# Graph attention layers of a GNN + FFN kernel on Trainium2: scores, softmax and edge sums joined into one stage of four chunks

## Chip, cores and metric

The kernel runs on one core of one Trainium2 chip. The metric is device time in microseconds (us) of one execution, the median of several.

## What is computed

A graph of 3125 nodes and 53,125 directed edges (sorted by destination) with 256 features per node passes through one attention layer, a routed FFN, three graph attention (GAT) layers with a small MLP behind them, and a second routed FFN. The change touches the three GAT layers. Their reference, cut to what matters:

```python
def _gat(x, src, dst, W, a_src, a_dst, b, heads, out_ch, concat):
    h = (x @ W).reshape(n, heads, out_ch)
    al_s = jnp.einsum('nhc,hc->nh', h, a_src)
    al_d = jnp.einsum('nhc,hc->nh', h, a_dst)
    e = jax.nn.leaky_relu(al_s[src] + al_d[dst], 0.2)
    emax = jax.ops.segment_max(e, dst, num_segments=n)
    ee = jnp.exp(e - emax[dst])
    denom = jax.ops.segment_sum(ee, dst, num_segments=n)
    alpha = ee / (denom[dst] + 1e-16)
    out = jax.ops.segment_sum(h[src] * alpha[:, :, None], dst, num_segments=n)
    ...
h = elu(_gat(x, ..., 4 heads of 128, concatenated))   # layer 1
h = elu(_gat(h, ..., 4 heads of 128, concatenated))   # layer 2
h = _gat(h, ..., 1 head of 256)                       # layer 3
```

## The kernel before

Nodes lie in 25 tiles of 128. Edges are cut into 232 items (ITEMS): an item is two sub-blocks of 128 edges whose destinations fall in one node tile, whose number stands in the table `item_tile`. Two consecutive items are called a pair here (116 pairs; `groups` in the code). Every GAT layer runs five phases, each with a barrier of all engines behind it: dense (node rows h and the scores of the nodes), scores, edges (which begins with the softmax), nodes, and then the next layer's dense phase.

**Scores** (`phase_gat_scores`, L1616), a rolled loop over the 116 pairs. Each engine works in its own order and they meet at semaphores. SP loads the low parts of the source and destination numbers, repeated on 128 partitions, four items at a time and four such buffers ahead (L1647). DVE compares them with the partition number to get one-hot matrices (L1739) and every second pair builds one-hots of the source tile (L1736). PE multiplies one-hots with the node scores, which are cut into three bf16 parts: 12 matmuls of 100 columns (25 tiles x 4 heads) for the sources (L1689) and 12 of 8 columns for the destination (L1693), on four PSUM banks and four further ones. The table of the destination tile is copied by POOL for one item (L1672) and by ACT for the other (L1708). DVE masks the 400 results (L1747) and reduces them (L1753); ACT copies the destination's scores (L1712).

**Softmax**, the head of `phase_gat_edges` (L1759): PE transposes all scores, DVE runs a segmented maximum forwards and backwards over 512 columns per head (L1863 to L1893), with PE transposes between for the carry over partitions, then DVE forms the shifted exponents (L1901 to L1910) and ACT takes exp (L1837). Meanwhile ACT clears `acc` (L1834), the 25 x 522 sums, and POOL starts the gathers.

**Edges**, an unrolled loop over the 232 items. POOL gathers 2 x 128 rows of the table in DRAM with two indirect DMAs an item (L1827) into a ring of 12 items (layer 3: 24), and waits for the sum of the item that had the slot. ACT writes the weights behind the rows (L1844) and weighs two of four heads (L1850); DVE weighs the other two (L1928) and builds the one-hots of the destinations every four items (L1922). PE sums the item with the one-hots (L1816): 2 pieces of 261 columns x 2 sub-blocks, fp32, for the 521 columns of layers 1 and 2 (512 features, 4 weights, 4 maxima, 1 flag); 1 piece of 259 in layer 3. DVE adds the sum to the item's node tile (L1937), three items behind, for which it first loads the tile's number into a register (L1932). Four sums may be open:

```python
            for t in range(ITEMS + LAG):        # DVE, LAG = 3
                if t < ITEMS:
                    weigh(t)
                if t >= LAG:
                    add(t - LAG)
```

No planner sets the order; on each engine it is that of the code.

## Time and profile before

| | us |
|---|---|
| median of 3 runs | 5496.4 |
| lowest, highest | 5494.01, 5509.8 |
| profiled execution: its own time | 5452.6 |
| profiled execution: span from first to last instruction | 5450.9 |

The page of the profile counts PE busy for 71% of the span, DVE for 53%, POOL for 41% and ACT for 33%. The three GAT layers lie between about 1800 and 4740 us of the span. Views used below: the windows view (busy time of each engine in a stretch), groups of instructions by line, timelines of one engine, waits, and one line's instructions. "DVEq" stands for instructions that DVE's sequencer carries out by itself, which don't count as busy. A number in parentheses after an x is a count.

### The profile page before, as it was taken

The numbers are of one execution on the slowest core, as the hardware profiler recorded it, in microseconds if no ns is written. First come the engines' busy times: TensorE is split into PE (matmuls) and PEld (weight loads), VectorE is DVE, ScalarE is ACT, GpSimd is POOL, SyncE is SP. The second block draws the span as 40 slices with busy tenths as digits, with TensorE's granted clock in tenths as the row PEclk, the third lists the DMA queues.
The fourth block names the chain that finished last, engine by engine and source line by source line (L and its number), as shares of the span: only waits on it lengthen the run. The fifth ranks groups of instructions, "written<-read, shape, count | busy, mean of one in ns | idle before, by whom it ended". The sixth has DMA issues, their size and how long they took to land. (4 is left out here: it accounts for less than half of the span.)

```text
span 5450.9 us, 85101 instructions
## 1 busy us (share of the span) xinstructions
PE 3889.5 (71%) x22668; PEld 3121.2 (57%) x22669; DVE 2871.4 (53%) x6524; ACT 1797.9 (33%) x5670; POOL 2234.9 (41%) x2473
## 2 busy tenths in 40 slices
PE   5577776887997684777778667777664443667996
PEld 3455555686886474656546656556563322456885
DVE  4577777432002696555567955555784443662112
ACT  0566675221221224444422254444230000021221
POOL 0656663002221025666611356666037777502221
PEclk9788888988998767888888678888856665778998
DMA  2666663004556464666634556665373333304555
GB/s 80 180 180 180 187 186 106 17 25 153 181 185 156 129 172 130 182 183 182 183 114 133 155 149 184 181 181 166 109 215 91 91 91 94 89 29 160 185 182 168
DMA packets 348485, 782.46 MB, mean 144 GB/s; under 512 B 52869, under 2 KB 156908, under 8 KB 339692
## 3 DMA queue, kind: packets, MB, share of 16 engines
q0 software_dynamic: 145920, 459.41, 29.5%
q1 hardware_dynamic: 202348, 320.55, 18.8%
q8 instruction: 88, 1.44, 0.1%
q14 instruction: 129, 1.06, 0.1%
HBM read 729.52 MB, written 50.26 MB: 143 GB/s over the span
## 5 line engine op out<-in xcount | busy, mean ns | idle before, releaser
L1827 POOL DMA_INDIRECT h<-h_table,src_of x1392 | 1420.3, 1020 | 665.8 <-issue 387.6
L1816 PE MATMUL ps<-h,gat_edges_work 128*128 128x261 f32 x3712 | 978.9, 428 | 381.8 <-DVE h L1928 259.4
L1816 PEld LDWEIGHTS ps<-h,gat_edges_work 128*128 128x128 f32 x3712 | 782.1, 214 | 578.4 <-DVE h L1928 205.9
L1937 DVE TENSOR_TENSOR acc<-acc,ps 128x522 f32 (+1 forms) x696 | 418.4, 601 | 919.0 <-remote 596.7
L1850 ACT ACTIVATE h<-h,gat_shared 128x128 f32<-128x128 f32 x1856 | 592.7, 390 | 655.5 <-DMA h<-h_table,src_of 637.2
L724 POOL DMA_INDIRECT edges_rows<-kv_table,src_of x464 | 456.3, 983 | 415.5 <-DVE edges_out_rows L823 160.6
L1816 PE MATMUL ps<-h,gat_edges_hot 128*128 128x259 f32 x928 | 314.9, 495 | 344.1 <-DVE h L1928 179.3
L1928 DVE TENSOR_TENSOR h<-h,gat_shared 128x512 f32<-128x512 f32 x696 | 481.3, 693 | 38.3 <-DMA h<-h_table,src_of 37.2
L1816 PEld LDWEIGHTS ps<-h,gat_edges_hot 128*128 128x128 f32 x928 | 204.7, 240 | 453.9 <-DVE h L1928 168.8
L1325 DVE TENSOR_TENSOR moe_experts_result<-ps,moe_experts_b 128x512 f32<-128x512 f32 x64 | 44.3, 692 | 788.9 <-PE ps L929 788.9
L918 PE MATMUL ps<-moe_experts_turned,moe_experts_w 128*128 128x256 f32 x2048 | 455.9, 381 | 0.0
L929 PE MATMUL ps<-moe_experts_w,acc 128*128 128x256 f32 x2048 | 452.2, 379 | 0.0
L968 ACT ACTIVATE acc<-ps,moe_experts_b 128x256 f32<-128x256 f32 x512 | 214.5, 470 | 691.5 <-PE ps L918 662.1
L1672 POOL COPY gat_scores_of_item<-gat_scores_parts 128x24 bf16 (+1 forms) x348 | 101.0, 290 | 801.5 <-issue 486.9
L929 PEld LDWEIGHTS ps<-moe_experts_w,acc 128*128 128x128 f32 x2048 | 389.1, 190 | 52.9
L918 PEld LDWEIGHTS ps<-moe_experts_turned,moe_experts_w 128*128 128x128 f32 x2048 | 387.5, 192 | 50.7
L788 PE MATMUL ps<-edges_out_rows,h 128*128 128x264 f32 x928 | 308.5, 464 | 126.3 <-DVE edges_out_rows L823 107.4
L1342 POOL DMA_INDIRECT picked_out<-moe_experts_result,moe_slot_out x128 | 125.1, 978 | 635.7 <-DVE moe_experts_result L1325 616.2
L1335 POOL DMA_INDIRECT moe_experts_rows<-normed,moe_slot_in x128 | 124.2, 970 | 636.6 <-POOLq L206 576.0
L778 PE MATMUL ps<-h 128*128 x928 | 294.2, 448 | 103.0 <-issue 70.3
L1689 PE MATMUL ps<-gat_scores_parts,gat_scores_hot 128*128 128x100 bf16 (+1 forms) x4176 | 280.6, 228 | 116.6 <-DVE gat_scores_hot L1739 79.1
L1844 ACT COPY h<-gat_shared 128x18 f32<-128x18 f32 (+1 forms) x696 | 131.2, 193 | 565.9 <-remote 315.7
(349 smaller groups left out, 5709.8 us busy)
## 6 DMA issues: line engine op xcount, KB each, us to landing
moe_experts_w<-in_L_ffn_W SPq DMA_DIRECT2D x128, 1024.0 KB
gat_scores_rows<-src_rows SPq DMA_DIRECT2D x174, 256.0 KB, 3.8
gat_scores_rows<-dst_rows SPq DMA_DIRECT2D x174, 256.0 KB, 4.4
h<-h_table,src_of POOLq DMA_INDIRECT x1392
edges_dst_row<-dst_rows SPq DMA_DIRECT2D x58, 256.0 KB
h_table<-h SPq DMA_DIRECT2D x10, 1280.0 KB
h<-h_table SPq DMA_DIRECT2D x10, 1280.0 KB
h<-picked_out SPq DMA_DIRECT2D x48, 256.0 KB, 3.7
```

The lines of the kernel that those rows point to most:

```text
L724: nc.gpsimd.indirect_dma_start(rows[:, r, s, :], None, k.kv_table, bass.IndirectOffsetOnAxis(ap=k.src_of[:, 2 * t + s:2 * t + s + 1], axis ...
L778: mm = nc.tensor.matmul(psq[r % S][:, s * C:(s + 1) * C], hot_t[:, r % SH, s * P:(s + 1) * P], row(k.h, n, 0, C), start=True, stop=True)
L788: mm = nc.tensor.matmul(pso[r % S][:, 0:W], hot[:, r % S, s * P:(s + 1) * P], out_rows[:, r % S, s, :], start=(s == 0), stop=(s == 1))
L918: mm = nc.tensor.matmul(psh[q][:, j % 2 * GROUP:j % 2 * GROUP + m], f.w1[:, w, b, j * P:(j + 1) * P], f.turned[:, slot, b, 0:m], start=(b ...
L929: mm = nc.tensor.matmul(pso[slot][:, s * C:(s + 1) * C], f.hidden[:, slot, j, s * P:(s + 1) * P], f.w2[:, w, j, :], start=(j == 0), stop=( ...
L968: last = act.activation(f.hidden[:, slot, j, 0:m], k.ps[2 + q][:, j % 2 * GROUP:j % 2 * GROUP + m], ACT.Gelu, bias=e(j))
L1689: nc.tensor.matmul(bank[slot][:, s * HT:(s + 1) * HT], hot[:, slot, 0, s * P:(s + 1) * P], parts[:, p, 0:HT], start=(p == 0), stop=(p == 2))
L1816: mm = nc.tensor.matmul(k.ps[t % S * 2 + q][:, 0:PIECE], hot[:, t // BATCH % 3, t % BATCH * 2 + e, :], g.rows[:, t % RING, e, q * PIECE:(q ...
L1827: nc.gpsimd.indirect_dma_start(g.rows[:, r, e, 0:W], None, g.table, bass.IndirectOffsetOnAxis(ap=k.src_of[:, 2 * t + e:2 * t + e + 1], axis=0)
L1850: last = act.mul(cols, cols, g.sums[:, 2 * t + e, h:h + 1])
L1928: v.tensor_tensor(heads(t, 0, by_dve), heads(t, 0, by_dve), alpha.to_broadcast([P, 2, by_dve, D]), ALU.mult).then_inc(weighed, 1)
L1937: v.tensor_tensor(acc, acc, k.psum[:, t % S * 2:t % S * 2 + PIECES, 0:PIECE], ALU.add).then_inc(added, 1)
```

## The change

The phases scores and edges of a layer become one phase, `phase_gat_layer`, with the same sums in another order. Its 232 items are cut into chunks of 64 (64, 64, 64, 40).

- **Front.** Before the first item, the 32 pairs of chunk 0 are scored and its softmax is run in 20 small steps, of which PE, ACT and DVE do parts in turn. ACT now clears `acc` before it copies the first table of a pair (L1828, L1797). It copies both tables of a pair; POOL copies none.
- **Loop.** While the items of a chunk are summed, the next chunk is scored: one pair in three of four iterations, so that 32 pairs take 43 items. One-hots are built two iterations ahead, PE multiplies in the iteration, and DVE takes the results two behind. The softmax of that chunk takes its 20 steps in the last 20 items. The weights stand in two halves that alternate by chunk.
- **Scores.** Two PSUM banks instead of eight, two row buffers instead of four, three one-hot buffers instead of four. DVE, not ACT, copies the destination's scores (L1872).
- **Sums.** Layers 1 and 2: PE sums 512 columns and then the 9 last ones apart, four items side by side in a bank of their own. DVE adds the 512 columns per item (L1989), and every four items the four tails of 9 columns, each behind its own register load (L1993, L1996). Layer 3 has no tail, six open sums instead of four, and LAG 5.
- **Between chunks.** A node whose edges lie in two chunks needs a maximum over both: the maximum so far is carried on, and at each of three boundaries DVE rescales one node tile of `acc` by a factor (about ten small operations, one exp on ACT and one matmul).
- All loops of the phase are unrolled.

The diff, cut to its core:

```diff
+    BATCH, HOTS, HS, NB = 4, 3, 3, 2
+    S = 4 if TAIL else 6
+    LAG = S - 1
+    CH, E = 64, P
+    CHUNKS, PAIRED = -(-ITEMS // CH), ITEMS // 2
...
+    def scored(t):
+        if t < 0:
+            c, j = 0, t + CH
+        else:
+            c, j = t // CH + 1, (3 * (t % CH) + 2) // 4 if t % 4 < 3 else CH
+        q = c * CH // 2 + j
+        return q if 0 <= j < CH // 2 and q < PAIRED else None
+    def softmax_step(t):
+        c, n = (0, t + CH // 2 - 1) if t < 0 else (t // CH + 1, t % CH - CH + 20)
+        return (c, n) if c < CHUNKS and 0 <= n < 20 else (c, None)
...
+            def sum_item(t):
+                if t % BATCH == 0:
+                    pe.wait_ge(marked, t // BATCH + 1)
+                pe.wait_ge(weighed, t + 1)
+                pe.wait_ge(scaled, t + 1)
+                if t >= S:
+                    pe.wait_ge(added, t - S + 1)
+                if TAIL and t % BATCH == 0 and t >= 2 * BATCH:
+                    pe.wait_ge(tails_added, t // BATCH - 1)
+                for e in range(2):
+                    mm = nc.tensor.matmul(k.ps[t % S][:, 0:MAIN], hot[:, t // BATCH % HOTS, t % BATCH * 2 + e, :],
+                                          g.rows[:, t % RING, e, 0:MAIN], start=(e == 0), stop=(e == 1))
+                if TAIL:
+                    for e in range(2):
+                        mm = nc.tensor.matmul(k.ps[S + t // BATCH % 2][:, t % BATCH * TAIL:(t % BATCH + 1) * TAIL],
+                                              hot[:, t // BATCH % HOTS, t % BATCH * 2 + e, :],
+                                              g.rows[:, t % RING, e, MAIN:FULL], start=(e == 0), stop=(e == 1))
+                mm.then_inc(summed, 1)
...
+            def products(q):
+                c = q // (CH // 2)
+                pe.wait_ge(lo_hots, q + 1)
+                pe.wait_ge(chosen, q + 1)
+                if q >= 2:
+                    pe.wait_ge(masked, q - 1)
+                    pe.wait_ge(dst_taken, q - 1)
+                if c >= 1:
+                    pe.wait_ge(maxed, c)
+                if c >= 2:
+                    pe.wait_ge(factored, c - 1)
...
+            pe.wait_ge(cut, 1)
+            for t in range(-CH, ITEMS):
+                if t >= 0:
+                    sum_item(t)
+                q = scored(t)
+                if q is not None:
+                    products(q)
+                c, n = softmax_step(t)
+                if n is not None:
+                    softmax(c, n)
...
+            def choose(q):
+                if q >= 4:
+                    act.wait_ge(made, q - 3)
+                for j in range(2):
+                    n = act.value_load(k.item_tile[0:1, 2 * q + j:2 * q + j + 1], min_val=0, max_val=TILES - 1)
+                    last = act.copy(of_item[:, q % 4, j, :, :], tables(n))
+                last.then_inc(chosen, 1)
...
+            act.wait_ge(cut, 1)
+            act.wait_ge(noughts, 1)
+            act.copy(k.acc[:, :, 0:FULL], nought[:].rearrange("p (t a) -> p t a", t=1).to_broadcast([P, TILES, FULL])).then_inc(cleared, 1)
+            for t in range(-CH - 2, ITEMS):
+                q = scored(t + 2)
+                if q is not None:
+                    choose(q)
...
+            def one_hots(q):
+                b, at = q // 2, q % 2
+                dve.wait_ge(row_in[b % NB], (b // NB + 1) * 32)
+                if q >= HS:
+                    dve.wait_ge(made, q - HS + 1)
+                if at == 0:
+                    v.tensor_tensor(tile_hot[:, b % 4], k.iota_row[:, 0:TILES].rearrange("p (a n) -> p a n", a=1).to_broadcast([P, 8, TILES]),
+                                    k.src_hi[:, 8 * b:8 * b + 8].rearrange("p (s a) -> p s a", a=1).to_broadcast([P, 8, TILES]),
+                                    ALU.is_equal)
+                v.tensor_scalar(lo_hot[:, q % HS, :, :], rows_lo[:, :, b % NB, at * 512:(at + 1) * 512], k.iota_p[:, 0:1], None,
+                                ALU.is_equal).then_inc(lo_hots, 1)
...
+            def take_scores(q):
+                b, at, j = q // 2, q % 2, 4 * (q % (CH // 2))
+                dve.wait_ge(lo_hots, q + 1)
+                dve.wait_ge(made, q + 1)
+                if q >= 2:
+                    dve.wait_ge(picks, q - 1)
+                v.tensor_tensor(picked[:, q % 2], bank[q % 2][:, 0:4 * HT].rearrange("p (s h n) -> p s h n", s=4, h=H),
+                                tile_hot[:, b % 4, at * 4:at * 4 + 4].rearrange("p s (a n) -> p s a n", a=1).to_broadcast([P, 4, H, TILES]),
+                                ALU.mult).then_inc(masked, 1)
+                v.tensor_copy(g.of_dst[:, :, j:j + 4], bank[q % 2][:, 4 * HT:4 * HT + 8 * H].rearrange("p (s h) -> p h s", s=4)
+                              ).then_inc(dst_taken, 1)
+                dve.wait_ge(masked, q + 1)
+                v.tensor_reduce(g.of_src[:, :, j:j + 4].rearrange("p h s -> p s h"), picked[:, q % 2], AX.X, ALU.add).then_inc(picks, 1)
...
+            def rescale(c):
+                n = dve.value_load(k.item_tile[0:1, c * CH:c * CH + 1], min_val=0, max_val=TILES - 1)
+                dve.wait_ge(factored, c)
+                dve.wait_ge(added, c * CH)
+                if TAIL:
+                    dve.wait_ge(tail_link, c * CH)
+                for h in range(H):
+                    v.tensor_scalar(row(k.acc, n, h * D, (h + 1) * D), row(k.acc, n, h * D, (h + 1) * D), factor[:, h:h + 1], None, ALU.mult
+                                    ).then_inc(rescaled, 1)
+                v.tensor_tensor(row(k.acc, n, W, W + H), row(k.acc, n, W, W + H), factor[:], ALU.mult).then_inc(rescaled, 1)
+                dve.wait_ge(rescaled, (H + 1) * c)
...
             def add(t):
+                if t == 0:
+                    dve.wait_ge(cleared, 1)
+                elif t % CH == 0:
+                    rescale(t // CH)
                 n = dve.value_load(k.item_tile[0:1, t:t + 1], min_val=0, max_val=TILES - 1)
                 dve.wait_ge(summed, t + 1)
                 if t:
                     dve.wait_ge(added, t)
-                acc = k.acc[:, bass.ds(n, 1), 0:PIECES * PIECE].rearrange("p a (q c) -> p (a q) c", q=PIECES)
-                v.tensor_tensor(acc, acc, k.psum[:, t % S * 2:t % S * 2 + PIECES, 0:PIECE], ALU.add).then_inc(added, 1)
-
-            for t in range(ITEMS + LAG):
-                if t < ITEMS:
+                v.tensor_tensor(row(k.acc, n, 0, MAIN), row(k.acc, n, 0, MAIN), k.ps[t % S][:, 0:MAIN], ALU.add).then_inc(added, 1)
+            def add_tails(b):
+                for i in range(BATCH):
+                    n = dve.value_load(k.item_tile[0:1, b * BATCH + i:b * BATCH + i + 1], min_val=0, max_val=TILES - 1)
+                    if b * BATCH + i:
+                        dve.wait_ge(tail_link, b * BATCH + i)
+                    v.tensor_tensor(row(k.acc, n, MAIN, FULL), row(k.acc, n, MAIN, FULL),
+                                    k.ps[S + b % 2][:, i * TAIL:(i + 1) * TAIL], ALU.add).then_inc(tail_link, 1)
+                dve.wait_ge(tail_link, BATCH * (b + 1))
+                dve.sem_inc(tails_added, 1)
+            for t in range(-CH - 2, ITEMS + LAG):
+                if 0 <= t < ITEMS:
                     weigh(t)
+                q = scored(t + 2)
+                if q is not None:
+                    one_hots(q)
+                q = scored(t - 2)
+                if q is not None:
+                    take_scores(q)
+                c, n = softmax_step(t)
+                if n is not None:
+                    softmax(c, n)
                 if t >= LAG:
                     add(t - LAG)
+                    if TAIL and (t - LAG) % BATCH == BATCH - 1:
+                        add_tails((t - LAG) // BATCH)
```

What stands in a row on DVE, in the loop of layers 1 and 2. `h` is the ring of gathered rows, `acc` the sums, `ps` PSUM, ISA a sequencer's instruction. Before, one item, weighed and (another, three behind) added:

```order
L1928 TENSOR_TENSOR h<-h,gat_shared 128x2x256
L1932 TENSOR_LOAD item_tile
L1932 ISA x2
L1937 ISA
L1937 TENSOR_TENSOR acc<-acc,ps 128x522
```

The same engine now, behind the weighing (L1965), in an iteration in which a pair is scored and four tails are due:

```order
L1860 TENSOR_SCALAR gat_layer_lo_hot<-gat_layer_rows_lo,iota_p 128x1024
L1869 TENSOR_TENSOR keys<-ps,gat_layer_tile_hot 128x400
L1872 COPY gat_shared<-ps 128x8x4
L1875 TENSOR_REDUCE keys<-keys 128x4x4
L1985 TENSOR_LOAD item_tile
L1985 ISA x2
L1989 ISA
L1989 TENSOR_TENSOR acc<-acc,ps 128x512
L1993 TENSOR_LOAD item_tile
L1993 ISA x2
L1996 ISA
L1996 TENSOR_TENSOR acc<-acc,ps 128x9
```

Between the weighing and the add stand the three steps of the pair (four with L1857 in every second pair); the last four rows stand there four times before the next weighing.

ACT at the start of the layer. Before, the clearing of `acc` stands behind the scores of the whole layer:

```order
L1708 COPY gat_scores_of_item<-gat_scores_parts 128x24
L1712 COPY gat_shared<-ps 128x8x4 x3
L203 UNCONDITIONAL_BRANCH
L1831 UNCONDITIONAL_BRANCH
L1834 COPY acc<-gat_edges_nought 128x25x522
```

Now:

```order
L1788 UNCONDITIONAL_BRANCH
L1828 COPY acc<-gat_layer_nought 128x25x521
L1797 TENSOR_LOAD item_tile
L1797 ISA x2
L1798 ISA
L1798 COPY gat_layer_of_item<-gat_layer_parts 128x24
```

The clearing has moved ahead of the first table, which PE needs for the first pair.

## Rows read from the trace of the kernel before

**Rows 1.** Windows view: window, its length, busy us (count) of each engine, PE clock, DMA.

```profile
core 0: us, PE busy (x) PEld busy (x) DVE busy (x) ACT busy (x) POOL busy (x), PEclk, DMA share, GB/s
1878.00:2053.00 175.00, 143.74 (x2784) 137.75 (x2784) 173.20 (x405) 47.52 (x229) 37.33 (x115) 0.69 0.64 169
2053.00:2112.00 59.00, 10.15 (x48) 8.03 (x48) 48.22 (x74) 19.17 (x9) 31.25 (x24) 0.53 0.38 107
2112.00:2766.00 654.00, 489.13 (x1848) 391.52 (x1849) 354.18 (x516) 316.50 (x1156) 434.85 (x440) 0.86 0.63 177
...
3942.00:4055.00 113.00, 89.28 (x2781) 83.38 (x2778) 104.46 (x404) 39.20 (x230) 28.57 (x112) 0.50 0.85 259
4055.00:4080.00 25.00, 5.05 (x24) 2.73 (x22) 17.42 (x31) 8.25 (x14) 19.52 (x18) 0.50 0.31 89
4080.00:4731.00 651.00, 314.94 (x928) 204.75 (x928) 294.95 (x521) 41.06 (x223) 465.75 (x447) 0.67 0.32 90
```

**Rows 2.** Windows view, two stretches of layer 3's edges: DVE nearly idle, DVE full.

```profile
4120.00:4170.00 50.00, 8.39 (x17) 4.74 (x17) 6.32 (x11) 0.98 (x5) 38.12 (x40) 0.50 0.36 104
4195.00:4219.00 24.00, 19.11 (x80) 13.19 (x78) 24.00 (x45) 3.77 (x20) 19.55 (x15) 1.00 0.29 83
```

**Rows 3.** Timeline, layer 3: start, us, engine, line, what [idle before <-releaser].

```profile
4158.71 2.10 PE L1816 MATMUL ps<-h,gat_edges_hot 128*128 128x259 f32 x4 [9.11 <-ACT h L1844]
4168.82 0.42 DVE L1937 TENSOR_TENSOR acc<-acc,ps 128x259 f32 x1 [10.17 <-remote]
```

**Rows 4.** Timeline of DVE in layer 1's edges, items at hand.

```profile
2500.47 0.69 DVE L1937 TENSOR_TENSOR acc<-acc,ps 128x522 f32 x1
2501.07 0.71 DVE L1928 TENSOR_TENSOR h<-h,gat_shared 128x512 f32<-128x512 f32 x1
2501.71 0.69 DVE L1937 TENSOR_TENSOR acc<-acc,ps 128x522 f32 x1
```

**Rows 5.** Line L1932, 2498 to 2500 us: durations min/median/max ns, first and last start.

```profile
L1932 DVEq TENSOR_LOAD <-item_tile x2: 300/301/302, 2498.2 to 2499.1; - x2
L1932 DVEq FUSED_REGOPS  x2: 190/190/190, 2498.5 to 2499.4; - x2
L1932 DVEq SEQ_ASSERT  x2: 23/23/23, 2498.8 to 2499.6; - x2
```

**Rows 6.** Groups by line, layer 1's scores: count, busy us, mean ns, idle before.

```profile
L1747 DVE TENSOR_TENSOR acc<-ps,acc 128x400 f32<-128x400 f32 x116 | 65.6, 566 | 0.7 <-PE ps L1693 0.5
L1753 DVE TENSOR_REDUCE keys<-acc 128x400 f32 (+1 forms) x116 | 64.7, 559 | 0.0
L1739 DVE TENSOR_SCALAR gat_scores_hot<-gat_scores_rows,iota_p 128x1024 bf16<-128x1024 bf16 x116 | 55.3, 477 | 0.0
L1736 DVE TENSOR_TENSOR acc<-iota_row,src_hi 128x200 f32<-128x200 f32 x57 | 20.2, 354 | 0.6 <-DMA gat_scores_rows<-dst_rows 0.6
```

**Rows 7.** Groups by line and form, whole span.

```profile
L1834 ACT COPY acc<-gat_edges_nought 128x13050 f32<-128x13050 f32 x2 | 22.1, 11070 | 6.0 <-DVE gat_edges_nought L1856 6.0
...
L1873 DVE COPY gat_edges_cin<-ps 128x16 f32<-128x16 f32 x1 | 0.2, 175 | 0.7 <-PE ps L1800 0.7
```

**Rows 8.** Timeline of PE: a pair's 24 matmuls at half clock and at full clock.

```profile
1904.44 1.08 PE L1689 MATMUL ps<-gat_scores_parts,gat_scores_hot 128*128 128x100 bf16 x12 [0.17 <-DVE gat_scores_hot L1739]
1905.36 0.44 PE L1693 MATMUL ps<-gat_scores_of_item,gat_scores_hot 128*128 128x8 bf16 x12
...
1907.24 0.70 PE L1689 MATMUL ps<-gat_scores_parts,gat_scores_hot 128*128 128x100 bf16 x12 [0.47 <-DVE gat_scores_hot L1739]
1907.78 0.45 PE L1693 MATMUL ps<-gat_scores_of_item,gat_scores_hot 128*128 128x8 bf16 x12
```

**Rows 9.** Timeline of PE in a dense phase at full clock: fp32, 8 and 512 columns.

```profile
2858.22 0.95 PE L606 MATMUL ps<-gat_wa,gat_shared 128*128 128x8 f32 x8
2859.50 3.60 PE L606 MATMUL ps<-gat_w,gat_shared 128*128 128x512 f32 x8
```

**Rows 10.** Groups by line, DVE, layer 1's edges.

```profile
L1922 DVE TENSOR_TENSOR gat_edges_work<-iota_row,dst_in 128x1024 f32<-128x1024 f32 x57 | 69.7, 1223 | 0.0
```

457 lines of the change are left out of this document (201 added, 256 removed).

## The prediction, made before the changed kernel ran

> **What bounds the kernel now.** I read the windows view first. A GAT layer of four heads spends 175 us on scores, 59 us on the softmax and 654 us on the edges; layer 3 spends 113, 25 and 651 us [rows 1]. Layer 2 I take as layer 1. The reader should see three different limits. In the scores DVE is busy for 173.2 of 175 us. In the softmax DVE is busy for 48.2 of 59, and the other 11 are hand-overs between PE and DVE. In the edges no engine is full: PE 489, DVE 354, POOL 435 of 654 us. POOL is still the nearest: at its full pace it issues 40 gathers in 50 us [rows 2], 1.25 us each, so 464 of them need 580 us. When DVE is busy without a break, 15 gathers take 24 us [rows 2], 1.6 us each. The rest of the 2.82 us per item is a delay between PE and its readers: PE's four matmuls of an item start at 4158.71 and last 2.10 us, yet DVE's next add, which waits for a sum of PE, starts at 4168.82 after 10.17 us of idleness [rows 3]. So DVE has 300 of 654 us to spare in the edges, and the change wants to put the 234 us ahead of them there.
>
> **The front, layers 1 and 2.** It holds 32 pairs and one softmax.
> - ACT's clearing of acc (11.07 us [rows 7]) stood under the softmax. It now stands ahead of the first table, and PE cannot begin without one: +13 us with the table's load and copy.
> - A pair cost 175/116 = 1.5 us, DVE's own work. Now two PSUM banks close a loop. DVE masks pair q (0.57 us [rows 6]) and copies the destination's scores (PSUM to SBUF, 0.175 [rows 7]), which frees the bank, 0.66 with overlap; PE starts 0.2 later and needs 1.0 us at full or 1.4 at half clock for 24 matmuls [rows 8]; only then may DVE build the next one-hots (0.48, and half of 0.35 [rows 6]), 0.55, and with 0.1 for the signal the next mask follows. That is 2.5 to 2.9 us a pair; I take 2.75, nearer the half clock, since PE waits half the time: 32 x 2.75 = 88 us. Bounds: 48 us at the old pace, 96 at 3.0.
> - Softmax of 128 columns: a quarter of 48 us, 2 us of fixed cost for forty small operations, the same 11 us of hand-overs, 1 for exp: 26 us.
> Together 127 us against 234: **-107 us** a layer.
>
> **The loop, layers 1 and 2.** DVE's work for four items:
> - Weighing and adding: two steps of 0.6 us (the adds start at 2500.47 and 2501.71 [rows 4]), 4 x 1.24 = 5.0 us.
> - The destination's one-hots, 1.22 [rows 10] less overlap: 1.15.
> - Four tails. The add of 9 columns itself is some 0.15 us. But each stands behind a load of the tile's number, of which the sequencer's parts take 0.30, 0.19 and 0.02 us, and two loads in a row start 0.9 us apart with nothing in their way (2498.2 and 2499.1 [rows 5]). Today this lies under the 0.7 us weighing. With four loads behind one another nothing is left for DVE to do: 4 x 0.88, less what the add of 512 columns covers, 3.1 us. Bounds: 0.7 if all is hidden, 3.7 if nothing.
> - Three pairs: 0.57 + 0.56 + 0.48 + 0.18 (half of L1736) + 0.17 (the copy that ACT made) [rows 6, 7] less overlap of 0.3 is 1.65 each, 5.0. The reduce waits for the mask, and the add's register load comes after it, 0.9 us against 0.6 of reduce: 0.3 each, 0.9.
> Sum 15.1 us, 3.75 an item while a pair is scored, and 9.2/4 = 2.3 while none is. PE needs 4 x (4 x 0.45 + 4 x 0.12) [rows 9] + 3 x 1.0 = 12.1 us at full clock, 14 at the 0.86 of these edges [rows 1], so it stays just behind DVE. ACT and SP gain work too, with room left: ACT had 316 of 654 us, and a pair adds two loads and two copies, about 2 us.
>
> The layer then: chunks 0 and 1, each 43 items x 3.75 = 161 us, and 21 x 2.3 = 48 with 25 for the softmax (14 of work, 8 of waits for PE, which answers only behind its item, 3 for the rescaling factor), 234 each, 468. Chunk 2: 27 x 3.75 = 101; 17 items at 2.9, POOL's pace beside a busy DVE, 49; 20 x 2.3 + 25 = 71; 221. Chunk 3: 40 x 2.95 = 118. Three rescalings of a tile, each with a stop until all adds are in, 9. Sum 816 us against 654: **+162 us**. With the front +55 a layer, **+110** for two.
>
> **Layer 3.** There is no tail. Front: clearing half as large, 7 us; a pair 1.9 us by the same loop with quarter-sized masks, 61; softmax 22; 90 against 138, -48. Loop: DVE needs under 2.4 us an item even with pairs, below POOL's 2.5, so POOL bounds. The moved work is 84 pairs of 104.5/116 = 0.9 us [rows 1] and 24 us of softmax, some 100 us of DVE; each busy us of DVE slows POOL by 1 - 1.25/1.6 = 0.22: +24, and +7 for rescaling. **-17 us.** Three barriers fall away, 2 us each: **-6 us.**
>
> Sum: 110 - 17 - 6 = **+87 us**. The profiled execution took 5452.6 us (span 5450.9) and the median is 5496.4; I add the change to both: 5540 profiled, 5583 as a median. I say **5580 us**.
>
> **The shared port.** In the rows POOL's gather goes from 1.25 to 1.6 us beside a full DVE [rows 2]; that is the price used above. The Trainium skill, SBUF — State Buffer, section "A bandwidth-pool intuition that's wrong", has a harder rule: a DVE operation that takes both ports locks POOL out of writing descriptors until it ends. By that rule it is the new one-hots in the loop (one source, bf16) that count, not DVE's total. The rows agree with a slowdown and don't show its form for this operation. As a mechanism here, each of 84 one-hots of 0.48 us [rows 6] that stops POOL adds 40 us a layer where POOL bounds, layer 3: rival E.
>
> **Rivals.**
> - **A (forecast, 0.52).** DVE bounds the loops of layers 1 and 2: 5580, own range 5500 to 5690.
> - **B (0.22), faster: the register loads are hidden.** If DVE has a backlog when the tails come, since PE or a gather was late, they cost 0.7 and not 3.1 us. Scoring items then take 3.2, the others POOL's 2.8 to 2.9: 199 + 199 + 192 + 112 + 9 = 711 us, 838 with the front, -50 a layer: 5496 - 100 - 23 = 5373. Against it: the tails stand behind the iteration in which DVE has most to do, and the loads 0.9 us apart are in the trace.
> - **C (0.07).** The front's pairs keep 1.5 us and the loops are as forecast: 2 x 40 and 30 in layer 3 less: 5470.
> - **D (0.13), slower still: the late signal of PE.** The 8 us in [rows 3] fell on an idle DVE. DVE now also waits in the same order for PE's products and transposes. If a delay of 8 us falls on one in five groups of four items, 1.5 us each, 58 groups in each of two layers give +175, and the front some 20: 5780. For it: every second wait of the softmax is of this kind. Against it: in stretches where DVE is busy and POOL slower the delay is not seen, and that is what the loop will be.
> - **E (0.06).** Descriptors starve in layer 3: 5620.
>
> **How the numbers follow.** The range leaves out at most the faster half of B and the slower half of D: 5385 to 5790. It takes in both bounds of the tail (0.7 to 3.7 us per four) together with those of the front. A change of 0.3%, 16 us, is about what a measurement can tell. Faster: B, most of C and a little of A, 0.26. Within: 0.10. Slower: 0.64. More of it is on the slow side because DVE alone, with no other wait, needs about 880 of today's 888 us of a layer: the former busy time of 173 + 48 + 354 = 575, 33 for copies and tails, 160 for the register loads, and the stops in front and softmax.
>
> **What the profile will show.** Right: the layers of four heads some 940 us from first pair to last add; DVE idle before the adds of 9 columns (L1996) for about 0.7 us each, put down to nothing that waits; pairs 2.5 to 2.9 us apart in the front; DVE idle before L1860 there, released by PE; 11 us without PE at the start. Wrong: adds of 9 columns back to back (then B), ring waits of POOL gone in layers 1 and 2, PE fuller than DVE in the loops, or idle DVE before L1869 and L1989 for 8 us at a time (then D). The forecast falls if the loop of layers 1 and 2 takes under 720 us.

## The result, and the profile of the changed kernel

The changed kernel takes 5674.2 us (median of 4 runs, 5652.27 to 5681.25), the kernel before 5503.1 (4 runs): a ratio of 1.030, 95% interval 1.0265 to 1.034. It is slower by 171 us where the prediction said 87: the direction was right, the size was half. The profiled execution took 5675.8 us. That of the kernel before had been 50 us below its median, so the two traces differ by 223 us; I read places from them, and the size from the medians.

Windows view of the changed kernel, one row each for the front (to the first weighing) and the loop of layers 1, 2 and 3. The answer to [rows 1].

```profile
core 0: us, PE busy (x) PEld busy (x) DVE busy (x) ACT busy (x) POOL busy (x), PEclk, DMA share, GB/s
1888.00:2028.00 140.00, 50.72 (x780) 46.95 (x780) 70.57 (x182) 28.00 (x70) 22.06 (x24) 0.50 0.41 112
2028.00:2886.00 858.00, 681.46 (x3914) 403.47 (x3914) 582.12 (x1266) 340.43 (x1331) 453.93 (x440) 0.88 0.56 160
3045.00:3185.00 140.00, 50.56 (x780) 46.96 (x780) 70.85 (x184) 26.82 (x69) 21.86 (x23) 0.50 0.37 113
3185.00:4053.00 868.00, 686.83 (x3914) 404.00 (x3914) 583.03 (x1265) 339.99 (x1331) 451.33 (x440) 0.88 0.55 158
4176.00:4312.00 136.00, 27.55 (x774) 24.40 (x774) 43.64 (x171) 18.55 (x70) 45.09 (x48) 0.50 0.44 117
4312.00:4954.00 642.00, 431.92 (x2968) 303.34 (x2968) 408.06 (x992) 60.37 (x403) 451.58 (x416) 0.67 0.42 119
```

Fronts: 140, 140, 136 (forecast 127, 127, 90). Loops: 858, 868, 642 (forecast 816, 816, 682). In no stage is an engine full: in the loop of layer 1 DVE works 582 of 858 us and PE 681. Two kinds of idleness fill the rest.

**The first is the one forecast.** DVE in layer 1's loop: the end of an iteration in which a pair is scored and four tails are due.

```profile
2115.22 0.69 DVE L1989 TENSOR_TENSOR acc<-acc,ps 128x512 f32 x1 [0.25 <-issue]
2116.02 0.17 DVE L1996 TENSOR_TENSOR acc<-acc,ps 128x9 f32 x1
2116.80 0.17 DVE L1996 TENSOR_TENSOR acc<-acc,ps 128x9 f32 x1 [0.61 <-DVE acc L1996]
2117.57 0.17 DVE L1996 TENSOR_TENSOR acc<-acc,ps 128x9 f32 x1 [0.61 <-DVE acc L1996]
2118.35 0.17 DVE L1996 TENSOR_TENSOR acc<-acc,ps 128x9 f32 x1 [0.61 <-issue]
2118.66 0.69 DVE L1965 TENSOR_TENSOR h<-h,gat_shared 128x512 f32<-128x512 f32 x1
```

Four additions of 0.17 us stand 0.78 us apart, behind their register loads.

**The second stands where no term of the forecast was.** Layer 3's front, timelines of PE, DVE and ACT, and the windows view of 47 us of it:

```profile
4182.80 0.27 PE L1748 MATMUL ps<-gat_layer_of_item,gat_layer_lo_hot 128*128 128x2 bf16 x5
4183.72 0.16 PE L1748 MATMUL ps<-gat_layer_of_item,gat_layer_lo_hot 128*128 128x2 bf16 x1 [0.64 <-issue]
4185.15 0.20 PE L1748 MATMUL ps<-gat_layer_of_item,gat_layer_lo_hot 128*128 128x2 bf16 x2 [1.28 <-issue]
4186.61 0.20 PE L1748 MATMUL ps<-gat_layer_of_item,gat_layer_lo_hot 128*128 128x2 bf16 x2 [1.26 <-issue]
4188.05 0.16 PE L1748 MATMUL ps<-gat_layer_of_item,gat_layer_lo_hot 128*128 128x2 bf16 x1 [1.23 <-issue]
4188.74 0.19 PE L1748 MATMUL ps<-gat_layer_of_item,gat_layer_lo_hot 128*128 128x2 bf16 x1 [0.53 <-issue]
4244.17 0.48 PE L1744 MATMUL ps<-gat_layer_parts,gat_layer_lo_hot 128*128 128x25 bf16 x12 [55.23 <-DVE gat_shared L1872]
```

```profile
4195.28 0.48 DVE L1860 TENSOR_SCALAR gat_layer_lo_hot<-gat_layer_rows_lo,iota_p 128x1024 bf16<-128x1024 bf16 x1 [12.77 <-remote]
4242.97 0.37 DVE L1857 TENSOR_TENSOR gat_layer_tile_hot<-iota_row,src_hi 128x200 f32<-128x200 f32 x1 [47.21 <-remote]
```

```profile
4195.82 0.20 ACT L1798 COPY gat_layer_of_item<-gat_layer_parts 128x6 bf16 x1 [13.51 <-remote]
...
4243.51 0.20 ACT L1798 COPY gat_layer_of_item<-gat_layer_parts 128x6 bf16 x1 [46.87 <-remote]
```

```profile
4188.00:4235.00 47.00, 0.35 (x2) 0.10 (x1) 0.48 (x1) 0.40 (x2) 35.72 (x38) 0.50 0.40 116
```

In the second pair PE's matmuls begin to come in ones and twos, every 1.4 us, with nothing named that they wait for, and DVE and ACT stand still for 47 us, until 4243. POOL meanwhile issues its 48 first gathers, one each 1.25 us; its last starts at 4234.46. The trace also has the time of every semaphore update. The first pair's last matmul is recorded at 4182.5 and its signal at 4195.2; the second pair's at 4188.7 and its signal at 4242.9, 54 us later and 7.5 us after the last gather has ended. Where between these two times PE really works the trace doesn't tell. I call this "PE held": the records of matmuls far apart, or their signal late. In layers 1 and 2, where the ring is 24 gathers long, the first masking comes 36 us after the phase's start.

### The profile page after: what moved, and what is told of

It is laid out like the page before. It is cut to its first block and busy times, and to the rows that moved or that the text cites. A ratio compares the mean times of both kernels' runs of the same rounds, so it can differ in the third digit from the quotient of the medians.

```text
span 5674.0 us, 83659 instructions
## 1 busy us (share of the span) xinstructions
PE 4132.1 (73%) x22686; PEld 2996.0 (53%) x22687; DVE 3057.7 (54%) x7636; ACT 1756.6 (31%) x5685; POOL 2162.9 (38%) x2124
## 5 line engine op out<-in xcount | busy, mean ns | idle before, releaser
L1706 POOL DMA_INDIRECT h<-h_table,src_of x1392 | 1448.6, 1041 | 1748.3 <-PE ps L1726 811.4
L1722 PE MATMUL ps<-h,gat_layer_hot 128*128 128x512 f32 (+1 forms) x2784 | 1445.3, 655 | 563.8 <-DVE h L1965 344.6
L1722 PEld LDWEIGHTS ps<-h,gat_layer_hot 128*128 128x128 f32 x2784 | 581.1, 231 | 938.9 <-issue 464.4
L1989 DVE TENSOR_TENSOR acc<-acc,ps 128x512 f32 (+1 forms) x696 | 414.9, 596 | 254.6 <-issue 126.7
L1965 DVE TENSOR_TENSOR h<-h,gat_shared 128x512 f32<-128x512 f32 x696 | 478.3, 688 | 30.2 <-DMA h<-h_table,src_of 11.8
L1798 ACT COPY gat_layer_of_item<-gat_layer_parts 128x24 bf16 (+1 forms) x696 | 145.9, 219 | 1104.5 <-PE ps L1748 465.0
L1726 PEld LDWEIGHTS ps<-h,gat_layer_hot 128*128 128x128 f32 x1856 | 321.6, 216 | 278.8 <-issue 278.8
L1744 PE MATMUL ps<-gat_layer_parts,gat_layer_lo_hot 128*128 128x100 bf16 (+1 forms) x4176 | 255.0, 215 | 252.3 <-DVE gat_shared L1872 147.8
L1744 PEld LDWEIGHTS ps<-gat_layer_parts,gat_layer_lo_hot 128*128 128x128 bf16 x4176 | 235.0, 113 | 288.2 <-DVE gat_layer_lo_hot L1860 195.5
L778 PEld LDWEIGHTS ps<-h 128*128 128x128 f32 x928 | 207.9, 232 | 188.8 <-issue 150.9
```

Of the source, the lines that this page charges most:

```text
L778: mm = nc.tensor.matmul(psq[r % S][:, s * C:(s + 1) * C], hot_t[:, r % SH, s * P:(s + 1) * P], row(k.h, n, 0, C), start=True, stop=True)
L1706: nc.gpsimd.indirect_dma_start(g.rows[:, r, e, 0:W], None, g.table, bass.IndirectOffsetOnAxis(ap=k.src_of[:, 2 * t + e:2 * t + e + 1], axis=0)
L1722: mm = nc.tensor.matmul(k.ps[t % S][:, 0:MAIN], hot[:, t // BATCH % HOTS, t % BATCH * 2 + e, :], g.rows[:, t % RING, e, 0:MAIN], start=(e ...
L1726: mm = nc.tensor.matmul(k.ps[S + t // BATCH % 2][:, t % BATCH * TAIL:(t % BATCH + 1) * TAIL], hot[:, t // BATCH % HOTS, t % BATCH * 2 + e, :],
L1744: nc.tensor.matmul(bank[q % 2][:, i * HT:(i + 1) * HT], lo_hot[:, q % HS, 0, i * P:(i + 1) * P], parts[:, p, 0:HT], start=(p == 0), stop=( ...
L1965: v.tensor_tensor(heads(t, 0, by_dve), heads(t, 0, by_dve), alpha.to_broadcast([P, 2, by_dve, D]), ALU.mult).then_inc(weighed, 1)
```

## Two kinds of batches

The experiments ran in six batches (the expectations say "call"), each with the kernel before in it and each on one chip. In four batches the kernel before took 5466 to 5510 us; I call them A, and the runs of the result (5503) are like them. In two it took 5176 and 5177: B. What differs isn't shown. It isn't simply which chip it is: e1, e2, e3 and e6 ran on the chip that the record numbers 4, in B, and 27 minutes later c2 and e1_again on number 4, in A. Groups by line, DVE, whole span: the same addition, in a phase ahead of the GAT layers that the change doesn't touch, in the changed kernel (A) and in e3 below (B).

```profile
L833 DVE TENSOR_TENSOR acc<-acc,ps 128x264 f32 x232 | 97.5, 420 | 157.3 <-issue 130.1 <-remote 20.8 <-DVE edges_out_rows L823 2.8
```

```profile
L833 DVE TENSOR_TENSOR acc<-acc,ps 128x264 f32 x232 | 97.3, 419 | 1.3 <-DVE acc L833 0.8 <-PE ps L788 0.5
```

157 us of waiting in A, 1.3 in B, at equal busy time: in B PE isn't held. The kinds give the experiments a second axis. No trace of the kernel before was taken in B. Front and loop of each layer in us, from DVE's first instruction of the phase to the first L1965 and from there to the last L1989 (the lines' own timelines):

| kernel | kind | ratio to before | layer 1 | layer 2 | layer 3 |
|---|---|---|---|---|---|
| changed | A | 1.030 | 142, 857 | 142, 868 | 137, 642 |
| e1_again: gathers behind front | A | 1.031 | 128, 880 | 128, 880 | 84, 703 |
| e2_again: tails without loads | A | 1.003 | 142, 787 | 141, 775 | 135, 635 |
| e6_again: four edits | A | 0.975 | 93, 775 | 93, 775 | 73, 648 |
| e1 | B | 1.017 | 128, 793 | 128, 788 | 86, 614 |
| e2 | B | 0.981 | 123, 720 | 124, 726 | 87, 576 |
| e3: six front banks | B | 0.997 | 98, 789 | 97, 789 | 77, 577 |
| e4: e1 and e2 | B | 0.991 | 128, 724 | 128, 723 | 84, 620 |
| e5: four edits, late gathers | B | 0.972 | 93, 723 | 92, 723 | 74, 616 |
| e6 | B | 0.968 | 93, 720 | 93, 727 | 72, 583 |

The changed kernel itself never ran in a batch of kind B. It can be estimated: e3's 5156 us plus the fronts of e2 in place of its own (25 + 28 + 10) is 5219; e1 and e2 corrected in the same way give 5213 and 5210. That is an estimate of some +40 us, 1.007 to 1.008, where A has +171.

## Experiments

**The kernels unchanged (c0, c1, c2, c3, c4).**

c0, the kernel before: 

> The kernel before, unchanged, for its trace beside the experiments, which ran at 5176 us for it where 5496 was measured first. Theory (in the first traces PE's signals came late whenever POOL issued gathers unbroken, and here they don't): the edges of layer 3 take 580 to 600 us instead of 651, bounded by POOL's 1.25 us a gather (464 x 1.25 = 580), and DVE has no idleness of 10 us before L1937. Rival (the difference is PE's granted clock alone, 0.86 against 0.82): edges of layer 3 at 640 or more with the same 10 us stops.

Measured: a batch of kind A, 5519.2 us; layer 3's edges 675 us and 39 stops of DVE of over 4 us before its adds, together 319 us. The delay of [rows 3] came in every trace of A. A third trace of the kernel before, c3 (5472 us, also A), has 32 such stops, 270 us.

c1, the changed kernel: 

> The changed kernel, unchanged, to stand beside the experiments on the same chip. If the ratio of 1.030 holds: 5330 us. If the late signals of PE made part of both kernels' times and hit the kernel before more, the ratio grows: fronts of 122 us, loops of 790 us in layers 1 and 2 and 580 in layer 3 give 5260 us, 1.016.

c2: 

> The changed kernel once more, in the same call as the next run. Where the kernel before takes 5499 us: 5664, the fronts' first masking 36, 36 and 69 us after their start. Where the kernel before takes 5176: first maskings 17, 17 and 13 us after the start, loops of 790, 790 and 577 us (as in the single edits), 5245 us, a ratio of 1.013; if the ratio is 1.029 there too, 5327, the late signals are no part of the loss.

c4: 

> The changed kernel in the same call. Where the kernel before takes about 5500 us: 5665. Where it takes 5176: from the stages of the single edits (fronts of 123, 124 and 87 us in e2, loops of 789, 789 and 577 us in e3) e3's time of 5156 plus 25, 28 and 10 us for the fronts, 5219, a ratio of 1.008.

Measured, all three in A: 5664, 5662 and 5673 us, ratios 1.029 (1.0265 to 1.0312), 1.030 (1.0281 to 1.0321) and 1.0315 (1.0279 to 1.0352). The result repeats to 0.3%. What was expected of c1 (5330 or 5260) was worked out for a batch like that of the first experiments, B, and it ran in A.

**e1: does POOL's burst hold PE?** One edit:

```diff
         def _(pool):
+            pool.wait_ge(exped, 1)
             for t in range(ITEMS):
```

In B: 

> The changed kernel with one edit: POOL waits for the exponentials of chunk 0 before its first gather, in each of the three layers. Theory (PE is held while POOL issues gathers one behind another and DVE stands still): the first masking (L1869) comes 14 us after the first one-hots of the front instead of 35 in layers 1 and 2 and instead of 60 in layer 3, so the fronts shrink from 140, 140 and 136 us to about 120, 120 and 80; some 5 us a layer come back at the first item, whose rows now arrive late. Sum about -80 us. Rival (the stop comes from something else at the start of the phase, such as the clearing or code that isn't there yet): the fronts stay and the kernel gets 15 us slower.

Measured: 5260.8 us, ratio 1.017 (1.015 to 1.0184). The first masking comes 17, 17 and 11 us after the start. But in e2 and e3 of the same batch, whose gathers start at once, it comes at 17, 17 and 13 us too: in B there was nothing to win, and layer 3's loop loses 37 us for its late rows (614 against 577).

In A, beside the unchanged kernel: 

> The changed kernel with POOL's first gather behind the exponentials of chunk 0, beside the unchanged one. Where the kernel before takes 5499 us, theory (unbroken gathers hold PE): first maskings 17, 17 and 11 us after the start, fronts 19 + 19 + 50 us shorter, 5664 - 85 = 5580. Rival (what delays PE there isn't POOL): 5680, fronts unchanged. Where the kernel before takes 5176: 15 us slower than the changed kernel, since the first rows only come later.

Measured: 5672.6 us, ratio 1.031, the changed kernel beside it 1.030. The time is the rival's, the fronts are the theory's: the first masking comes at 17, 17 and 11 us, and the fronts are shorter by 14, 14 and 53 us. What neither foresaw is that the loops grew by 26, 15 and 62 (c2's are 854, 864, 641). Windows view of e1_again, layer 3's front and the 72 us behind it, and DVE in these:

```profile
4177.00:4261.00 84.00, 26.88 (x774) 23.91 (x774) 44.50 (x178) 19.86 (x77) 5.18 (x4) 0.50 0.46 125
4261.00:4333.00 72.00, 16.68 (x116) 10.29 (x116) 7.96 (x21) 1.29 (x8) 49.64 (x51) 0.52 0.35 101
```

```profile
4283.10 0.41 DVE L1858 TENSOR_TENSOR gat_layer_tile_hot<-iota_row,src_hi 128x200 f32<-128x200 f32 x1 [14.04 <-remote]
...
4332.21 0.49 DVE L1861 TENSOR_SCALAR gat_layer_lo_hot<-gat_layer_rows_lo,iota_p 128x1024 bf16<-128x1024 bf16 x1 [46.09 <-remote]
```

The stops of 13 and 47 us went with the burst: 14 and 46 us, now at the first items. So in A the burst makes them, and moving it moves them. In B the same burst of 48 gathers, 1.25 us apart and beside an idle DVE (layer 3's front in e3), makes none.

**e9, e10: does DVE's idleness belong to it?** 40 needless compares on DVE, first behind DVE's first wait for PE (e9, at `q == 0` ahead of the first masking), then ahead of it (e10, shown):

```diff
+                if q == 3:
+                    for i in range(40):
+                        if i >= 3:
+                            dve.wait_ge(busy, i - 2)
+                        v.tensor_tensor(hot[:, i % 3], ..., ALU.is_equal).then_inc(busy, 1)
                 if q is not None:
                     one_hots(q)
```

e9: 

> The changed kernel with 40 needless compares of 1024 columns (1.2 us each, 47 us) on DVE ahead of the first masking of every layer, while POOL issues its first gathers. Where the kernel before takes 5499 us: ACT's fifth table (it waits for PE's first pair) comes 22, 22 and 14 us after the fourth now, the seventh (it waits for the second pair) 1.2, 1.2 and 48 us after the fifth. Theory (PE is held only while DVE is idle): both come within 3 us, since DVE is busy. Rival (POOL's burst holds PE whatever DVE does): they come as late as now, or later still, since POOL is slower beside a busy DVE: its 48 gathers last 77 instead of 60 us. Time: 3 x 47 less what the stops took (19 + 19 + 56), 5710, or 5790 to 5820 by the rival. Where the kernel before takes 5176 the tables come within 3 us anyway.

Measured: 5778.5 us, both stops as before (12.9 and 46.2 us in layer 3). It tells nothing: the fourth pair's one-hots (L1861 there) wait for PE and stand ahead of the compares, so these ran when the burst was over.

e10: 

> The changed kernel with 40 needless compares of 1024 columns on DVE, 47 us, now right behind the third one-hots of every front and so ahead of DVE's first wait for PE, while POOL issues its first gathers. What is read: when ACT copies the tables of the fifth pair (they wait for PE's first pair) and of the sixth (PE's second pair). In the changed kernel, where the kernel before takes 5499 us, they come 22 and 23 us after those of the fourth pair in layers 1 and 2, 14 and 61 us after in layer 3. Theory (PE is held while DVE is idle): both within 3 us of the fourth pair's. Rival (POOL's burst holds PE whatever DVE does): both at 15 us or later, in layer 3 the sixth at 50 us or later. Where the kernel before takes 5176 they come within 3 us in any case.

Measured, in A beside c4, one run: 5701.2 us. After the fourth pair's last table those of the fifth and sixth pairs come at 1.7 and 3.2 us (layer 1), 1.7 and 3.0 (layer 2), 4.5 and 5.8 (layer 3); in c4 at 21.5 and 22.7, 21.6 and 22.8, 17.1 and 61.3. Three of the six are past the 3 us that the theory asked for, but all are far from the rival's 15. Layer 3 of e10, DVE and ACT, and a window in which the compares run:

```profile
4198.21 45.49 DVE L2010 TENSOR_TENSOR gat_layer_hot<-iota_row,dst_in 128x1024 f32<-128x1024 f32 x40
```

```profile
4202.16 0.20 ACT L1799 COPY gat_layer_of_item<-gat_layer_parts 128x6 bf16 x1 [4.30 <-PE ps L1749]
4202.78 0.20 ACT L1799 COPY gat_layer_of_item<-gat_layer_parts 128x6 bf16 x1 [0.42 <-issue]
4203.42 0.20 ACT L1799 COPY gat_layer_of_item<-gat_layer_parts 128x6 bf16 x1 [0.43 <-issue]
```

```profile
4199.00:4247.00 48.00, 1.41 (x31) 1.11 (x30) 46.32 (x46) 0.80 (x4) 41.30 (x23) 0.50 0.25 71
```

While DVE computes no signal of PE comes late; ACT no longer waits 47 us. Three times 45.5 us of needless work, 136, cost 28. In layer 3 the same front shows the other half as well. The compares end at 4243.7 with 22 gathers still to come, POOL goes on at 1.25 us each until 4270, and DVE, idle again, stands for 22 us until PE's next signal:

```profile
4271.52 0.37 DVE L1858 TENSOR_TENSOR gat_layer_tile_hot<-iota_row,src_hi 128x200 f32<-128x200 f32 x1 [22.43 <-remote]
```

So the theory holds for the fronts: in A, PE is held while POOL gathers unbroken **and** DVE is idle. One rival stands beside it. The compares slow POOL down: while they run its gathers stand 2.27 us apart, not 1.25, which is twice the 1.14 us of one compare (the window's 23 in 48 us take in three behind them). The slower pace, and not DVE's work as such, may be what frees PE; no run has one without the other. The Trainium skill, SBUF — State Buffer, section "A bandwidth-pool intuition that's wrong", has POOL blocked from writing descriptors until a DVE copy releases the port that the two share. The compares here are another operation, with two sources, so their effect on POOL is a measurement of its own and no test of that rule. What a burst does to PE no run explains; only when.

**b1: short pauses in POOL, in the kernel before.**

```diff
+                if t % 2:
+                    nc.gpsimd.memset(pause[:], 0.0).then_inc(paused, 1)
+                    pool.wait_ge(paused, t // 2 + 1)
```

b1: 

> The kernel before with one edit: after every second item POOL writes a small tile of 128 columns and waits for it, a pause in its chain of gathers. Where PE's signals are late because POOL issues without a break: DVE's stops of 10 us before L1937 vanish in layer 3 and the edges there take 600 to 630 us instead of 651, 50 us less in all. Where they are not late at all, POOL's added 0.3 to 0.5 us per two items only cost: 116 x 0.4 = 46 us in layer 3 and up to as much in layers 1 and 2, up to 140 us slower.

Measured, in A: 5522.5 us, ratio 1.003 (1.0015 to 1.0051). POOL's timeline in layer 3's edges:

```profile
4147.15 0.94 POOL L1828 DMA_INDIRECT h<-h_table,src_of  x1 [0.30 <-issue]
4148.10 0.22 POOL L1832 MEMSET gat_edges_pause<- 128x128 f32 x1
4148.59 0.95 POOL L1828 DMA_INDIRECT h<-h_table,src_of  x1 [0.27 <-issue]
```

The memset and its wait add 0.2 us to every fourth spacing of two gathers (1.44 for 1.25). Stops of over 4 us in layer 3: 37 for c0's 39, 305 us for 319, while c3 without any pause has 270. A pause that short and that rare frees nothing that can be seen, and costs 0.3%. It leaves open what a longer one would do.

**e2: the tails' register loads.** The registers of the four adds of 512 columns are kept and used again:

```diff
-                    n = dve.value_load(k.item_tile[0:1, b * BATCH + i:b * BATCH + i + 1], ...)
+                    n = of_tile[i]
```

In B: 

> The changed kernel with one edit: the four adds of 9 columns use the registers that the four adds of 512 columns loaded, so four register loads fall away in every group of four items. Theory (the loads stand alone on DVE's path): the 0.61 us of idleness before each L1996 goes, 2.4 us less per four items wherever DVE bounds, that is for some 190 of the 232 items: 48 groups x 2.4 = 115 us a layer, 230 in all if PE doesn't become the bound; since PE needs 12 us of the 15.6 for four items, I expect 150 to 230 us less. Rival (PE and the exchange between DVE and PE set the pace, the loads lie beside a wait for PE): less than 60 us.

Measured, in B: 5078.4 us, ratio 0.981 (0.9797 to 0.983), some 135 us below the estimate for the changed kernel; the loops go from 789 to 720 and 726.

In A: 

> The tails without register loads, alone. Where the kernel before takes 5499 us: 2.4 us less per four items where DVE bounds. If late signals take nothing of it, the same 70 us a layer as where PE is not held (loops of 790 down to 723), in two layers 140 to 160 less: 5510, ratio 1.002. If PE's late signals grow as DVE gets idle: 80 less, 5585. Where the kernel before takes 5176: 0.981 again.

Measured, in A: 5486.3 us, ratio 1.003 (1.0018 to 1.0047). The loops go from 857 and 868 to 787 and 775. DVE's timeline of e2_again, and the group of the tails in the changed kernel and in e2_again:

```profile
2113.64 0.69 DVE L1989 TENSOR_TENSOR acc<-acc,ps 128x512 f32 x1 [0.25 <-issue]
2114.25 1.08 DVE L1999 TENSOR_TENSOR acc<-acc,ps 128x9 f32 x4
2115.48 0.69 DVE L1965 TENSOR_TENSOR h<-h,gat_shared 128x512 f32<-128x512 f32 x1
```

```profile
L1996 DVE TENSOR_TENSOR acc<-acc,ps 128x9 f32 x464 | 76.4, 165 | 225.7 <-DVE acc L1996 137.1 <-issue 81.2
```

```profile
L1999 DVE TENSOR_TENSOR acc<-acc,ps 128x9 f32 x464 | 76.0, 164 | 51.8 <-issue 2.0 <-DVE acc L1999 1.3
```

From the add to the next weighing 1.84 us for 3.44; 174 us of idleness gone in all. Without these loads the change is at +0.3% in A and -1.9% in B: 2.7% of the time in A, 145 us, and about the same in B, hung on one line.

**e3: the loop of two banks.** In the front the products rotate over `k.ps[q % 6]`.

e3: 

> The changed kernel with one edit: in the front (chunk 0) the products rotate over six PSUM banks, which hold sums only later, instead of two. Theory (two banks close a loop between DVE and PE): pairs come 1.7 us apart instead of 2.71 in layers 1 and 2 and about 1.2 instead of 1.79 in layer 3, 31 x 1.0 = 31 us a layer and 18 in layer 3, together -80 us. Rival (PE at half clock or the three one-hot buffers bound the pairs): less than 25 us in all.

Measured, in B: 5156.4 us, ratio 0.997 (0.9954 to 0.9979). From first to 32nd masking 59, 58 and 51 us against 84, 86 and 62 in e2: in layers 1 and 2 1.9 us a pair for 2.7. The fronts are 63 us shorter in all, where 80 were expected. Rival C (1.5 us a pair in the front) is refuted: the changed kernel takes 2.7, and even with six banks it would be 1.9.

**e8: the pairs.** The loop's scoring left out (`return q if t < 0 ...`).

e8: 

> The changed kernel without the scoring of chunks 1 to 3: their pairs are left out, the softmax of each chunk runs on the scores of chunk 0, so the sums are not the reference's. Theory (in 113 of 232 items DVE's added work sets the pace): these items take 2.4 instead of 3.95 us in layers 1 and 2, 175 us less a layer, and 2.5 instead of 3.1 in layer 3, 65 less: 5250 us where the changed kernel takes 5664. Rival (PE and its late signals set the pace and the pairs fill gaps): under 200 us less in all, items at 3 us and more.

Measured, in B, one run: 4841.9 us, some 373 below the estimate. Items take 2.2 us where they took 3.7, in layers 1 and 2, 113 items each; loops of 613 and 619 us. The pair's price of 1.5 us an item is the forecast's (3.75 - 2.3). The 20 steps of the softmax still take 21 items at 3.75, 32 us more than items without. Layer 3's loop is 553 us for e3's 577: 24 us less, where 65 were expected.

**e4, e5, e6: together.** e4 is e1 and e2; e5 adds the six banks and the clearing of `acc` behind the last table of the front; e6 has, instead of POOL's wait for the exponentials:

```diff
                 if t >= RING:
                     pool.wait_ge(summed, t - RING + 1)
+                else:
+                    pool.wait_ge(made, min(2 * t + 4, CH // 2))
```

e4: 

> The changed kernel with two edits: POOL begins its gathers behind the exponentials of chunk 0, and the tails use the registers already loaded. Where PE's signals come late beside unbroken gathers (a time of 5499 us for the kernel before): the first masking of a front comes 17 us after its start instead of 36, 36 and 69, which gives back 19 + 19 + 56 us, less 5 a layer at the first item; the tails give 200; 5664 - 80 - 200 = 5385 us. If instead the late start of the fronts has nothing to do with POOL, the first masking stays at 36 and 69 us and the time is 5480. Where the signals are not late (5176 us for the kernel before): e2's time and 10 to 15 us more, 5090.

e5: 

> The four edits together (tails without register loads, six banks in the front, clearing behind the last table, gathers behind the exponentials of chunk 0). Beside the version with gathers spread over the front (ratio 0.968 to the kernel before where signals are not late): 1.5% slower at most from the first items' late rows, 0.970 to 0.975. Where PE's signals are late, the gathers beside the front no longer hold it: 5664 - 80 (fronts) - 200 (tails) - 80 (banks) - 30 (clearing) = 5275 us, 0.96 of the kernel before. If late signals fill what the tails give back in the loops, 5380, 0.98.

e6: 

> The changed kernel with four edits: no register loads for the tails, six banks in the front, the clearing of acc behind the last table of the front instead of ahead of the first, and POOL's first ring of gathers spread over the front (item t waits for 2t+4 finished pairs). If the terms are independent: 190 + 80 + 3 x 12 + 75 = 380 us less than the changed kernel, 5290, faster than the kernel before by 4%. If PE bounds the loops once DVE has room, some 100 less of that, 5390.

Measured, all in B: e4 5131.1 us, 0.991 (0.9894 to 0.9927); e5 5030.6, 0.972 (0.9702 to 0.9735); e6 5007.4, 0.968 (0.9664 to 0.9696). The terms add up: the estimate of 5219 less 141 for the tails (e2), 63 for the banks (e3) and 3 x 5 for the clearing is 5000, e6 has 5007. The clearing was worth 5 us a layer (first masking at 11.4 for 16.8), not the 12 expected. Late gathers cost more than expected: e4 takes 53 us more than e2, where 10 to 15 were foreseen, and 44 of them are layer 3's loop (620 for 576).

In A: 

> The four edits with POOL's first ring of gathers spread over the front, item t behind 2t+4 finished pairs. Where the kernel before takes 5499 us: no unbroken burst stands in the front or at the first items, so the fronts are as where PE is not held (93, 93 and 72 us against 142, 142 and 136) and the first sum comes some 14 us behind the first weighing: -49 -49 -64 = -160; tails -150 to -230 in the loops: 5664 - 160 - 190 = 5310, ratio 0.965. If the delay only moves into the loops, as it did when all gathers came behind the front: 5664 - 130 (banks, clearing) - 190 = 5340 to 5400, 0.975. Where the kernel before takes 5176: 0.968 again.

Measured, in A: 5330.9 us, 0.975 (0.9721 to 0.9779): the fronts are those of the first case, the time is that of the second. Its windows of layer 1's and layer 3's front and loop:

```profile
1873.00:1966.00 93.00, 49.35 (x780) 45.37 (x780) 70.72 (x189) 28.78 (x70) 23.62 (x24) 0.52 0.57 171
1966.00:2741.00 775.00, 638.41 (x3914) 383.76 (x3914) 580.28 (x1265) 340.14 (x1331) 455.16 (x440) 0.93 0.62 177
3886.00:3959.00 73.00, 28.36 (x774) 24.27 (x774) 43.07 (x175) 19.05 (x68) 37.43 (x39) 0.50 0.70 198
3959.00:4607.00 648.00, 431.22 (x2968) 302.79 (x2968) 406.51 (x993) 60.64 (x404) 455.75 (x426) 0.67 0.43 120
```

In A the fronts are now those of B: with the gathers spread over the front no stop is left there. The loops stay 48 to 65 us longer than B's. PE's clock doesn't explain that, as layer 2's loop shows in e6 (B) and e6_again (A), at the same granted clock and with PE busy for only 6 us more:

```profile
2781.00:3508.00 727.00, 624.77 (x3914) 377.73 (x3914) 579.99 (x1265) 341.61 (x1331) 458.23 (x440) 0.94 0.65 189
2989.00:3765.00 776.00, 630.48 (x3914) 380.03 (x3914) 580.25 (x1266) 340.46 (x1332) 454.30 (x440) 0.94 0.61 177
```

This version beats both kernels in both kinds.

## Why the prediction was right or wrong

- **What failed: "in stretches where DVE is busy and POOL slower the delay is not seen, and that is what the loop will be"**, the sentence that kept rival D at 0.13 and its price out of the sum. Its first half is right as far as e10 goes. Its second isn't: DVE is busy for 582 of 858 us of the loop, and at the start of a front it stands idle from the third pair on, just when POOL empties its ring at full pace. What the held PE costs by A against B: the fronts 19, 18 and 50 us (142, 142, 137 in A against 123, 124, 87 in B), the loops 68, 79 and 65 (857, 868, 642 against 789, 789, 577).
- **That the loops' part is late signals too**, their records show. A signal of PE is late here when it comes more than 1 us after the end that the profile models for its matmul. In the changed kernel's loops 99 of 322 signals are late, 105 of 323 and 134 of 289, by 207, 212 and 366 us together; in e3's loops, in B, none of 336, 337 and 319. DVE is at work for only 0.52, 0.43 and 0.48 of that time, but at work: unlike in the fronts, some signals are late beside a busy DVE. PE's lower clock (0.88 against 0.93) can be in the loops' excess as well, at most by the 36 and 42 us that PE is busy longer in layers 1 and 2; e6 and e6_again have the excess without it.
- **The change's share.** The kernel before has such stops as well (41, 38 and 30 of over 4 us before the adds of its three layers, in the first trace). The estimate for B leaves +40 of the +171, so some 130 us are what the held PE takes from the changed kernel beyond what it took from the one before. That is an estimate, and it holds if nothing else parts A from B.
- **The signs.** Rival D's, stops of 8 us before L1869 and L1989, didn't show in the loops of layers 1 and 2: the longest are 2.9 and 4.5 us. The delay came in many small pieces there (24 and 29 stops of DVE of over 2 us, 69 and 79 us; e3 has 4 and 4, 14 and 13) and in long ones in the fronts. A layer of four heads took 1000 and 1010 us where some 940 were foreseen.
- **Forecast A by its own terms.** Where PE isn't held its +87 would have been about +40: too high. A pair in the front: 2.75 forecast, 2.7 measured (2006.2 less 1922.2 over 31). An item while scoring: 3.75 forecast, 3.7 to 3.8 in B, 4.0 to 4.2 in A. Items while nothing is scored: 2.3 forecast, 2.2 to 2.3 in B, 2.6 to 2.8 in A. The softmax's 21 items: 73 forecast, 78 to 84 measured in either kind. Chunk 3: 118 forecast by POOL's pace, 102 and 106 in A, 88 in B (39 of its 40 items): POOL wasn't the bound there.
- **Tails.** 3.1 us per four items forecast. Without their loads four items take 1.7 us less while scoring (3.74 to 3.32 an item) and 0.5 less at the end (2.24 to 2.11) in B: the loads cost 1.2 us per four over a whole layer, since PE is close behind (619 of 720 us busy in e2's loop). Rival B (loads hidden, 5373) is refuted by the 0.61 us before each L1996.
- **Clearing.** +13 forecast, +5 measured; what else delays the first pair lay under it.
- **Layer 3.** -17 forecast, -11 between the traces (778 us for 789), from two misses: the front +46 (held PE), the loop 40 us shorter than forecast, and 105 in B. The forecast had started from 651 us of the trace before, which hold that kernel's own stops. Where nothing is held POOL does bound this loop, and its slowing by a busy DVE came as forecast. In e3 the 416 gathers of the loop follow one another without a wait and take 1.05 us each for the 0.95 of the front, 43 us more together; without pairs (e8) they take 20 us more. The pairs' 23 us are the +24 of the sum and the whole of the loop's 24 us (577 for 553). Rival E (descriptors starved by the new one-hots, 40 us more) isn't in it.
- **Sum.** The stages' errors are +13 + 13 for the fronts and +42 + 52 for the loops of layers 1 and 2, +46 and -40 in layer 3: 126 us, so 213 of the 223 us between the traces. 50 of these are the profiled execution of before, which was lower than its median. The 2 us taken for each barrier stand in no row; the trace before shows DVE idle for 0.85 us at one.

What stays open: what makes a batch A or B, by what path a gathering POOL holds PE, and whether it is DVE's work or POOL's slower pace that frees it.

## What to carry to other kernels

An engine that loads a register for each small operation pays for it (here 0.78 us for 0.17 us of work) once nothing long stands between; load once and keep it. Moving work under a loop with idle time takes only what the delay there leaves: name its cause before counting the idle time as room. Spread a burst of gathers over the work that it is issued beside: in this kernel that took the stops out of the fronts, where moving the whole burst had only moved them.
